# The first stage of a graph layer in another order: K's bias stored as rows, loads on two queues, two tiles by terms

## What is computed

```python
xn = _layernorm(x)
v = split_heads(xn @ Wv.T + bv)
k = split_heads(xn @ Wk.T + bk)
k_prime = relu(einsum('bhsd,hmd->bhsm', k, P)) / sqrt(M)
kv = einsum('bhsm,bhsd->bhmd', k_prime, v)
```

## Time and profile before

| | us |
|---|---|
| median of 3 runs | 1112.64 |
| lowest and highest run | 1112.21, 1113.32 |
| the profiled execution | 1114.37 |
| its span | 1112.3 |
| PE (TensorE) busy | 1088.9, 98% |
| DVE (VectorE) busy | 373.1, 34% |
| ACT (ScalarE) busy | 252.0, 23% |
| POOL (GpSimd) busy | 294.7, 26% |

### The profile page before, as it was taken

One profiled execution on the slowest core, in us unless ns is written; L12 is line 12 of the kernel. 1 busy time (PEld: TensorE's weight loads), 2 busy tenths in 40 slices (PEclk: granted clock), 3 DMA queues, 4 the chain that ended last, 5 costly groups with the idle time before them and its releaser, 6 DMA issues.

```text
span 1112.3 us, 14951 instructions
## 1 busy us (share of the span) xinstructions
PE 1088.9 (98%) x5630; PEld 903.9 (81%) x5630; DVE 373.1 (34%) x993; ACT 252.0 (23%) x397; POOL 294.7 (26%) x246
## 2 busy tenths in 40 slices
PE   5989999999999999999999999999999999999998
PEld 4778778888778888888878888887888888888887
DVE  6664566676641111322212213435321111111111
ACT  4331111111232345311111113334121111112000
POOL 4000011121133246400034554443132233225000
PEclk9999999999999999999999999999999999999999
DMA  6513001222234387604179987874022222216321
GB/s 243 114 30 105 7 19 59 71 61 69 65 122 143 127 299 247 216 1 152 38 218 328 294 243 210 226 208 147 1 86 62 61 61 61 71 52 219 109 98 67
DMA packets 146858, 139.29 MB, mean 125 GB/s; under 512 B 8974, under 2 KB 116834, under 8 KB 146530
## 3 DMA queue, kind: packets, MB, share of 16 engines
q1 hardware_dynamic: 146210, 136.21, 39.7%
q10 hardware_dynamic: 576, 2.10, 0.5%
HBM read 102.32 MB, written 35.96 MB: 124 GB/s over the span
## 4 chain that ended last, share of the span: by engine, by line
PE 95%; DMA 2%; DVE 2%; ACT 1%; issue 0%; SPq 0%; ACTq 0%; DVEq 0%
PE ps L1564 10%; PE ps L1565 9%; PE ps L1566 9%; PE ps L1824 7%; PE ps L1825 7%; PE ps L1826 7%; PE ps L1766 4%; PE ps L1760 4%; PE ps L1740 3%; PE ps L1691 3%; PE ps L1872 3%; PE ps L1741 3%; PE ps L1742 3%; PE ps L1870 3%; PE ps L1692 3%; PE ps L1693 3%
## 5 line engine op out<-in xcount | busy, mean ns | idle before, releaser
L1564 PE MATMUL ps<-w_hi,xnH 128*128 128x512 f32 x480 | 192.5, 401 | 0.0
L1566 PE MATMUL ps<-w_hi,xnL 128*128 128x512 f32 x480 | 188.1, 392 | 0.0
L1565 PE MATMUL ps<-w_lo,xnH 128*128 128x512 f32 x480 | 188.1, 392 | 0.0
L1564 PEld LDWEIGHTS ps<-w_hi,xnH 128*128 128x128 f32 x480 | 91.0, 190 | 19.5
L1566 PEld LDWEIGHTS ps<-w_hi,xnL 128*128 128x128 f32 x480 | 90.8, 189 | 19.6
L1565 PEld LDWEIGHTS ps<-w_lo,xnH 128*128 128x128 f32 x480 | 91.0, 190 | 17.9
L733 POOL TENSOR_TENSOR acc<-acc,cw 128x320 f32<-128x320 f32 x40 | 35.7, 894 | 262.6 <-ACT cw L912 261.5
L1519 DVE TENSOR_TENSOR prd<-ps,wB 128x512 f32<-128x512 f32 (+1 forms) x24 | 14.2, 592 | 162.6 <-PE ps L1826 148.4
L1691 PE MATMUL ps<-xnH,w_hi 128*128 128x512 f32 (+1 forms) x192 | 68.1, 355 | 0.0
L1824 PE MATMUL ps<-x2H,guH 128*128 128x512 f32 (+1 forms) x192 | 67.6, 352 | 0.4 <-ACT wT L1092 0.4
L1825 PE MATMUL ps<-x2L,guH 128*128 128x512 f32 (+1 forms) x192 | 67.6, 352 | 0.0
(11 more groups left out here) (304 smaller groups left out, 2042.1 us busy)
## 6 DMA issues: line engine op xcount, KB each, us to landing
cR<-c_d SPq DMA_DIRECT2D x20, 640.0 KB, 5.1
foldin<-in SPq DMA_DIRECT2D x32, 256.0 KB, 2.8
guR<-in SPq DMA_DIRECT2D x16, 512.0 KB, 5.1
c_d<-cw SPq DMA_DIRECT2D x40, 160.0 KB
w_raw<-in SPq DMA_DIRECT2D x12, 512.0 KB, 6.1
xb<-in SPq DMA_DIRECT2D x10, 512.0 KB, 6.1
qs0H<-qT_d SPq DMA_DIRECT2D x10, 512.0 KB, 5.5
qs0L<-qT_d SPq DMA_DIRECT2D x10, 512.0 KB, 6.8
```

The lines of the kernel that those rows point to most:

```text
L1564: pe.matmul(target, xnH[:, kc, cols], wH[w][:, kc, :], start=(kc == 0), stop=False)
L1565: pe.matmul(target, xnH[:, kc, cols], wL[w][:, kc, :], start=False, stop=False)
L1566: mm = pe.matmul(target, xnL[:, kc, cols], wH[w][:, kc, :], start=False, stop=(kc == KC - 1))
```

## The change

- SP loads the left half of tile 0 and ACT the right half, at the head of their queues. Then SP issues x 1 and weight pieces 1 and 3, ACT pieces 0 and 2 and x 2.
- ACT normalises the left half of tile 0, DVE the right half (new semaphore `xn_right`). ACT's list is reordered so that the first panel piece, x_hi, and the square roots alternate.
- PE starts with 26 transposes of `ident` into an unused bank. The first two tiles of V are multiplied by `products`, which takes one term over a range of blocks at a time; each matmul waits for just its operands. The order of transposes and terms is written out.
- DVE takes tile 0's x_low in two parts, and `v_out(0, 0)` stands ahead of the statistics of tile 4. `edges_convert` and `edges_keys` move to steps 1 and 2.
- K's folded bias is turned: PE transposes `bkf` (`folded_row`, with tile 2), ACT copies eight rows of 128 values to `fbr`, and SP stores those. In SP's list this stands after x 6 to 8 and folds 2 and 3; the load of `kbb` goes behind all folds of the stage.

```diff
+WARM = 26
 def load_x(t):
     if t >= 3: sp.wait_ge(xn_done, t - 2)
+    if t == 3: sp.wait_ge(xn_right, 1)
...
-for t in range(3):
-    load_x(t)
+sp.dma_start(xb[:, 0, 0:W], x[0][:, 0:W]).then_inc(in_x[0], 16)
+load_x(1)
+first_panel(sp, 1)
+first_panel(sp, 3)
...
-sp.wait_ge(bias_ev, 2)
-    sp.dma_start(fb_d.rearrange("o (c q) -> q (o c)", q=P), bkf[:]).then_inc(fb_st, 16)
-load_x(6)
-load_fold(0, 2)
+for kc in range(2, KC):
+    if kc + 4 < NT:
+        load_x(kc + 4)
+    if kc == 4:
+        sp.wait_ge(bias_ev, 3)
+        sp.dma_start(fb_d.rearrange("o (c q) -> (o c) q", q=P), fbr[:]).then_inc(fb_st, 16)
+    load_fold(0, kc)
 sp.wait_ge(fb_st, 16)
 sp.dma_start(kbb[:], fb_d[:, 0:W].to_broadcast([P, W])).then_inc(in_kb, 16)
-for kc in range(3, KC):
-    if kc + 4 < NT:
-        load_x(kc + 4)
-    load_fold(0, kc)
...
+act.dma_start(xb[:, 0, W:D], x[0][:, W:D]).then_inc(in_x[0], 16)
+first_panel(act, 0)
+first_panel(act, 2)
+act.dma_start(xb[:, 2, :], x[2]).then_inc(in_x[2], 16)
 ln1_sqrt(0)
+ln1_out(0)
 panel_hi(0, 0, 1)
-ln1_out(0)
+x_hi(0, 0)
+ln1_sqrt(1)
 panel_hi(0, 1, 1)
-ln1_sqrt(1)
+x_hi(0, 1)
+panel_hi(0, 2, 1)
 ln1_out(1)
-for h in range(2):
-    x_hi(0, h)
-panel_hi(0, 2, 1)
+ln1_sqrt(2)
 panel_hi(0, 3, 1)
-ln1_sqrt(2)
...
+if t == 2:
+    act.wait_ge(bias_mm, 2)
+    act.activation(fbr[:], bank(5)[0:KC, P:2 * P], ACT.Copy).then_inc(bias_ev, 1)
...
-edges = {0: (edges_convert,), 1: (edges_keys,), 3: ...
+edges = {1: (edges_convert,), 2: (edges_keys,), 3: ...
+ln1_stats(0)
+ln1_finish(0)
+dve.wait_ge(ln_step, LN_STEPS)
+dve.tensor_scalar(xn[:, 0, W:D], xb[:, 0, W:D], lnw[:, 0, 18:19], lnw[:, 0, 19:20], ALU.mult, ALU.add)\
+   .then_inc(xn_right, 1)
+ln1_stats(1)
+x_low(0, (0,))
+ln1_finish(1)
+x_low(0, (1,))
+ln1_stats(2)
+ln1_finish(2)
+x_low(1)
 ln1_stats(3)
-for t in range(NT):
+ln1_finish(3)
+x_low(2)
+v_out(0, 0)
+ln1_stats(4)
+for t in range(1, NT):
...
+for k in range(WARM):
+    pe.transpose(bank(7)[:, 0:P], ident[:], ident[:])
+transposes(0)
+for k in range(3):
+    products(0, ("hH", "lH"), (2 * k, 2 * k + 1))
+transposes(1)
+products(0, ("hL",), range(0, 4))
+products(0, ("hH", "lH"), (6, 7))
+products(1, ("hH",), range(KC))
+products(0, ("hL",), (4, 5))
+transposes(2)
+products(1, ("lH",), range(KC))
+products(0, ("hL",), (6, 7))
+products(1, ("hL",), range(KC))
+for t in range(1, NT):
...
+    if t >= 2:
+        rows(("v", 0, t), t, 0)
...
+    if t == 2:
+        folded_row()
```

More of the change, by code:

```diff
@@ L163, in gps_layer @@
             ("ktmp", [P, 2, W], F32), ("rest1", [P, 2, P], F16), ("rest2", [P, 2, SRCG], F16)), OY, OP)
-        (iota, iotaW, key1, key2, qmask, rowid, chunk, first2, share, rng, bvb, kbb, bkq, bkf,
+        (iota, iotaW, key1, key2, qmask, rowid, chunk, first2, share, rng, bvb, kbb, bkq, bkf, fbr,
          acc) = lay_out((
@@ L169, in gps_layer @@
             ("rng", [1, NWIN, 2], I32), ("bvb", [P, W], F32), ("kbb", [P, W], F32), ("bkq", [P, 2, KC], F32),
-            ("bkf", [P, KC], F32), ("acc", [P, SRCG], F32)), OP, OC)
+            ("bkf", [P, KC], F32), ("fbr", [KC, P], F32), ("acc", [P, SRCG], F32)), OP, OC)
         qF = [at(f"qF{c}", [P, QW[c]], F32, OY + 4096 * c) for c in range(3)]
@@ L293, in gps_layer @@
         xn_done = sem("xn_done")
+        xn_right = sem("xn_right")
         t1_done = sem("t1_done")
@@ L385, in fold_index, with first_panel @@
             return f * KC + kc
+        def first_panel(engine, piece):
+            cols = slice(piece * 2 * W, (piece + 1) * 2 * W)
+            engine.dma_start(wR[0][:].rearrange("q k n -> q (k n)")[:, cols], wv_pan[0][:, cols])\
+                .then_inc(in_w[0][piece], 16)
         block = ctx.enter_context(nc.Block())
@@ L857, in ln1_out @@
                     act.wait_ge(t1_done, 2 * (t - 1))
-                act.activation(xn[:, t % 2, :], xb[:, t % 3, :], ACT.Identity, scale=lnw[:, t % 2, 18:19],
+                cols = slice(0, D if t else W)
+                act.activation(xn[:, t % 2, cols], xb[:, t % 3, cols], ACT.Identity, scale=lnw[:, t % 2, 18:19],
                                bias=lnw[:, t % 2, 19:20]).then_inc(xn_done, 1)
@@ L1153, in ln1_finish, with x_low @@
                    .then_inc(ln_step, 1)
-            def x_low(t):
-                for h in range(2):
+            def x_low(t, halves=range(2)):
+                for h in halves:
                     dve.wait_ge(xh_done, 2 * t + h + 1)
@@ L1237, in edges_row @@
                 assert es[0] == EDGE_STEPS
-            edges = {0: (edges_convert,), 1: (edges_keys,), 3: (edges_reach, lambda: edges_inside(0)),
+            edges = {1: (edges_convert,), 2: (edges_keys,), 3: (edges_reach, lambda: edges_inside(0)),
                      4: (lambda: edges_inside(1),), 5: (edges_ends,), 6: (edges_row,)}
[L1242 to L1246, removed]
-            ln1_stats(3)
-            for t in range(NT):
+            ln1_stats(0)
[10 more added lines that the diff above has]
+            x_low(1)
+            ln1_stats(3)
+            ln1_finish(3)
[3 more added lines that the diff above has]
+            for t in range(1, NT):
                 if t + 3 < NT:
@@ L1543, in transposes @@
                 for h in range(2):
+                    if t == 0 and h == 1:
+                        pe.wait_ge(xn_right, 1)
                     if t >= 2:
@@ L1582, in folded_biases, with folded_row @@
                 mm.then_inc(bias_mm, 1)
+            def folded_row():
+                pe.wait_ge(bias_ev, 2)
+                pe.transpose(bank(5)[0:KC, P:2 * P], bkf[:], ident[:]).then_inc(bias_mm, 1)
             def chunk_windows():
                 pe.wait_ge(edge_step, EDGE_MIN)
-                pe.wait_ge(bias_ev, 2)
                 for a, m in enumerate((d5F, dmin)):
@@ L1605, in range_row, with products @@
                 mm.then_inc(range_mm, 1)
-            for t in range(2):
-                transposes(t)
-            for t in range(NT):
+            def products(t, terms, kcs):
+                target, cols = job_bank(("v", 0, t)), slice(t * P, (t + 1) * P)
+                for x_half, w_half in terms:
+                    for kc in kcs:
+                        if w_half == "H":
+                            pe.wait_ge(pan_hi, kc // 2 + 1)
+                        else:
+                            pe.wait_ge(pan_lo, kc // 2 + 1)
+                        if x_half == "h":
+                            pe.wait_ge(xh_done, 2 * t + kc // 4 + 1)
+                        else:
+                            pe.wait_ge(xl_done, 2 * t + kc // 4 + 1)
+                        last = w_half == "L" and kc == KC - 1
+                        mm = pe.matmul(target, (xnH if x_half == "h" else xnL)[:, kc, cols],
+                                       (wH if w_half == "H" else wL)[0][:, kc, :],
+                                       start=((x_half, w_half, kc) == ("h", "H", 0)), stop=last)
+                        if last:
+                            mm.then_inc(mm_done, 1)
+            for k in range(WARM):
[13 more added lines that the diff above has]
+            for t in range(1, NT):
                 if t in (3, 5, 6):
                     {3: chunk_windows, 5: window_chunks, 6: range_row}[t]()
-                rows(("v", 0, t), t, 0, ready=0 if t == 0 else None)
+                if t >= 2:
+                    rows(("v", 0, t), t, 0)
                 if t + 2 < NT:
```

9 lines of the change are left out of this document (4 added, 5 removed).

## The result

| us | before | after |
|---|---|---|
| median | 1112.98 (4 runs, 1112.21 to 1113.77) | 1103.53 (4 runs, 1102.44 to 1104.75) |
| the profiled execution, its span | 1114.37, 1112.3 | 1104.36, 1102.6 |
| start of tile 3's transposes | 29.53 | 24.43 |
| start of tile 8's transposes | 76.23 | 64.85 |

The ratio of after to before is 0.9915, with a 95% interval of 0.9898 to 0.9932: 9.45 us faster. 11.6 was forecast. The four executions of the changed kernel fall into two pairs, with spans of 1100.7 and 1100.9, and of 1102.6 and 1102.9; the median lies between them.

The account below looks back on a forecast made before the run. PE was taken as the bound, busy 1088.9 of 1112.3 us, so only its waits and low-clock work could go. Start 5.1 plus middle 6.5 made 11.6, from a median of 1112.64 to 1101.0; range 1098.9 to 1104.4.

Parts of the forecast that it names:

- The start, 5.1 us: First stage: earlier landing of tile 0 and reordered work bring tile 3's transposes from 29.53 to 24.4, 5.1 us gained.
- (D): Start: tile 0's halves bring nothing, ACT's chain starts 1.3 later, 1102.3; counted among the forecast's near variants, together 0.72.
- rival (A): Start: gaps between 8.7 and 14.35 keep or bring the low clock level; 2.7 us lost, 1103.7; chance 0.13.
- The middle, 6.5 us: From 29.53 to 76.23: 7.2 us removed, less 0.15 for the added transpose and 0.5 of remaining wait, 6.5 us gained.
- rival (B): Middle: DVE bounds for longer, wait before `window_chunks` 2 us and more; 1102.5 to 1103, or 1104.5; chance 0.10.
- The 7.2 us of waits and low clock: From 29.53 to 76.23: PE's idle of 2.2, 0.3 and 2.7, holes of 0.6, and matmuls and transposes at low level.
- The rest unchanged: Sign of a right forecast: after tile 8's transposes, expected near 64.6, the remaining work keeps its length.
- a later stage whose length changes: Sign of a wrong forecast: some stage behind the changed ones takes a different time than before; no size given.
- From the profiled execution to the median: Last term: the old median lay 1.7 below its profiled execution, so the new median was put at 1101.0.
- The twin: The changed kernel's counterpart of the profiled execution of before: 1102.8 us with a span of 1100.7.
- Rival (C): First stage and past it: low clock stays, each matmul costs 0.20 more, slower than before, up to 1117.8; chance 0.02.

## Why the prediction was right, and where it wasn't

- **The start, 5.1 us: right, step by step, but for the clock.** The first statistics at 4.64 (forecast 4.7), tile 1's transposes at 14.38 (14.35), tile 3's at 24.43 (24.4), against the earlier trace rows 5.10 gained. ACT was the chain as told, with one wait of 0.46 us for a weight piece. DVE's half of xn took 0.55 us, within its bounds. The rival on halves that bring nothing (D) is refuted by the kernel with tile 0 in one load, 1.77 us later.
- **The clock at the start: right result, wrong reason, and some luck.** The level was high at 14.35, so the price of rival (A) wasn't paid. But the text gave that to the 26 transposes, and in the execution without them it is high all the same; and with them it falls between 8 and 14 us in three of the seven executions with this start. So the first half of (A) did come there. Its cost did not, because the level was back before ACT's chain let go of PE. The text had the gaps down as harmless by their length (1.1 to 2 us behind the warm-up; they were 1.15 to 2.42); what made them harmless is that PE was waiting anyway. Without the twelve matmuls in terms, the 4.01 us of idle bring the low level to the work behind 14 us, and that costs. The Trainium skill, TensorE: Matmul & The Clock Gate, section A second HAM failure mode, made (A) the forecast; gaps of 0.43, 0.17 and 0.25 us between the first groups left the level high in the changed kernel's trace, three other traces of the same start show the fall, and none of them a cost over 0.4 us.
- **The middle, 6.5 us: right, 0.2 too much.** The stretch from tile 3 to tile 8 takes 40.42 where the earlier trace rows give 46.70, so 6.28 was gained. PE's wait before `cx` was 0.78 and not 0.5, since DVE had it ready at 51.19 and not 50.9; rival (B) came true in this small size only. The 7.2 us of waits and low clock was the right term (7.25 with the old start), and tile 8 was at 64.85, where 64.6 was forecast.
- **What in the middle brings it: not told apart.** The text treated the row form and the late place as one event and was right that the late place hides either form. It didn't say that the row form alone would do as well.
- **"The rest unchanged": the step that failed in the profiled execution.** To 779 us it holds within 0.05, and behind 800 us as well. Between them the clock fell behind the logits and cost 1.6: "a later stage whose length changes" was named as a sign of a wrong prediction, with no price and no chance. Nothing in the rows of before spoke for it, since the same block of small matmuls left the clock at 1.00 there.
- **From the profiled execution to the median: the other step that failed.** The twin was forecast at a span of 1100.7, and the two executions with a clock of 1.00 have 1100.7 and 1100.9, at 1102.44 and 1102.69 us. The text then took 1.7 us off for the median, as if the changed kernel's runs had to lie below their profiled twin as those of before did. They don't, and nothing had said that they would: the kernel before spreads over 3.4 us of span (1109.7 to 1113.1 over all its runs), and its profiled execution was one of the longer ones, with no fall behind the logits; what makes the others shorter, no run shows. Of the 2.5 us between 1101.0 and the median of 1103.53, this shift makes 1.6; the rest comes with the two longer executions.
- **Rival (C)** had no part in it: no stretch of the first stage stayed at the low level in the changed kernel's profiles.

## What to carry to other kernels

When an engine waits for a load, look at what stands ahead of it in the queue that issues it; a slow transfer costs nothing once nothing that is soon needed is queued behind it, and then its own form need not be mended. Parts of a change that move work into an idle stretch don't add up with the part that removes the stretch: measure each alone and all together. Set the forecast of a median against several executions, and give a price to a fall of the clock at every block of small matmuls.

## What the runs showed of the hardware

- 20 matmuls of 16 rows by 8 columns, 2.39 us in which PE counts as busy, were followed by a clock of 0.50 for about 3 us in three of eleven profiled executions, and not in the others: 1.6 us.
- The granted clock of the windows doesn't show the low level at the very start of a kernel: eight transposes took 1.94 us at 8.78 without warm-up, while the windows there say 1.00. After an idle stretch of 4.0 us it does show (0.50).
- PE idle for 4.01 us, behind eight transposes at the high level, brought the low level; then it lasted 5.6 us of steady work. Shorter gaps brought it in some executions and not in others: 2.21 us did at 8.66 in one kernel with the new start, and 2.42 us at the same place did not in another.
- Without warm-up the level was up some 3 us after PE's first work; in the changed kernel 5.70 us of transposes all ran at the low pace.
- Storing 4 KB as 1024 elements took 11.0 to 11.9 us in four kernels, and as 8 rows under 1.3 us, with 1024 packets fewer.
- A change between small and full matmuls costs PE 0.25 us for each group.
